# Five engines' written-out orders and the PSUM bank numbers replaced; partial maxima in two buffers

## The reference

```
h   = group_norm(x, 8 groups)
out = softmax(q k^T / sqrt(128)) v          # layer 0: one head of 128, 1024 x 1024
x   = x + proj(out)                         # t: tokens x 128
n   = layer_norm(t)
a   = softmax(sq sk^T / 4)                  # layer 1: 8 heads of 16, 1024 x 1024 each
ret = a @ rv (2 retrievers)                 # then a softmax over the 2 retrievers picks
t   = t + mix(ret) @ w_out
t   = t + layer_norm(t) @ dequant(qidx, scales)^T @ W^T
```

## Time and profile before

| | |
|---|---|
| median of 3 runs | 5282.57 us (5280.07 to 5285.5) |
| the profiled execution's own time | 5286.65 us |
| its span, first to last instruction | 5284.9 us |
| granted TensorE clock, mean | 0.971 |
| TensorE busy (matmuls) | 4855.4 us, 92% |
| GpSimd busy | 4245.3 us, 80% |
| VectorE busy | 3929.6 us, 74% |
| ScalarE busy | 3329.0 us, 63% |

### The profile page before, as it was taken

One profiled execution on the slowest core, in us unless ns is written; L12 is line 12 of the kernel. 1 busy time (PEld: TensorE's weight loads), 2 busy tenths in 40 slices (PEclk: granted clock), 3 DMA queues, 4 the chain that ended last, 5 costly groups with the idle time before them and its releaser, 6 DMA issues.

```text
span 5284.9 us, 102244 instructions
## 1 busy us (share of the span) xinstructions
PE 4855.4 (92%) x29838; PEld 2544.0 (48%) x29838; DVE 3929.6 (74%) x8176; ACT 3329.0 (63%) x6657; POOL 4245.3 (80%) x1173
## 2 busy tenths in 40 slices
...
GB/s 18 41 41 33 40 34 36 42 41 33 38 36 42 37 41 33 39 36 43 36 41 33 41 33 45 34 41 33 41 33 45 33 41 33 41 33 45 29 37 5
DMA packets 92849, 192.46 MB, mean 36 GB/s; under 512 B 16744, under 2 KB 50920, under 8 KB 92400
## 3 DMA queue, kind: packets, MB, share of 16 engines
...
...
## 4 chain that ended last, share of the span: by engine, by line
PE 58%; issue 18%; POOL 8%; ACT 7%; DVE 6%; ACTq 0%; DMA 0%; POOLq 0%; SPq 0%; DVEq 0%
PE ps_u L798 12%; PE ps_bank L749 8%; PE ps_bank L785 8%; POOL p_sum L639 8%; PE ps_bank L763 7%; ACT p L956 5%; DVE max_part L1057 3%; PE ps_bank L684 3%; PE ps_bank L673 3%; PE ps_bank L704 3%; PE ps_bank L735 2%; PE ps_bank L715 2%; PE ps_bank L807 2%; PE ps_bank L693 1%; PE ps_bank L738 1%
## 5 line engine op out<-in xcount | busy, mean ns | idle before, releaser
L639 POOL TENSOR_TENSOR p_sum<-p_sum,p 128x2048 f32<-128x2048 f32 x768 | 3500.6, 4558 | 176.5 <-ACT p L956 120.9
L1057 DVE TENSOR_REDUCE max_part<-ps_bank 128x1 f32<-128x512 f32 x4096 | 2615.0, 683 | 887.7 <-PE ps_bank L763 871.8
L956 ACT ACTIVATE p<-ps_bank 128x512 f32<-128x512 f32 x4096 | 2220.0, 601 | 1137.2 <-PE ps_bank L785 1111.8
L639 POOL TENSOR_TENSOR p_sum<-p 128x2048 f32<-128x2048 f32 x128 | 583.6, 4559 | 729.9 <-ACT den_sb L967 663.2
L798 PE MATMUL ps_u<-p,rv 128*32 128x512 f32 x8192 | 1050.3, 633 | 30.9 <-ACT p L956 30.9
L785 PE MATMUL ps_bank<-q_stack,k_stack 64*128 64x512 f32 x4096 | 952.9, 468 | 108.2 <-ACT p L956 57.7
L763 PE MATMUL ps_bank<-k_stack,q_stack 63*128 63x512 f32 x4096 | 935.8, 458 | 99.3 <-ACT p L956 66.6
L785 PEld LDWEIGHTS ps_bank<-q_stack,k_stack 64*128 64x128 f32 x4096 | 385.9, 186 | 722.8 <-issue 343.0
L763 PEld LDWEIGHTS ps_bank<-k_stack,q_stack 63*128 63x128 f32 x4096 | 390.0, 187 | 598.0 <-ACT p L956 238.4
L749 PE MATMUL ps_bank<-v,p 128*128 128x129 f32 x4096 | 521.8, 280 | 8.4 <-ACT p L956 7.0
L749 PEld LDWEIGHTS ps_bank<-v,p 128*128 128x128 f32 x4096 | 477.2, 191 | 85.2 <-issue 44.0
...
## 6 DMA issues: line engine op xcount, KB each, us to landing
...
k_stack<-k_lo SPq DMA_DIRECT2D x128, 128.0 KB, 2.7
q_stack<-q_lo SPq DMA_DIRECT2D x128, 128.0 KB, 2.8
...
```

What stands on the lines that cost most here:

```text
L639: pool.tensor_tensor(p_sum[:, :, :], before, p1[:, step % ring, :, :], ALU.add)\
L956: act.activation(p1[:, step % ring, n, :], bank_of("scores", index // 2, n % 2), ACT.Exp, scale=scale1)\
L1057: dve.tensor_reduce(max_part1[:, i, n, half:half + 1], bank_of("max1", index // 2, side), AXIS.X, ALU.max)\
```

## The change

All five lists are replaced. The entries are the same, one for one; their sequence, some images ahead and all bank numbers differ. Between two `den` entries TensorE's list holds:

| quarter | before | after |
|---|---|---|
| A | 31 pairs in 16 unbroken runs, 4 values, 3 value0, 7 score0, 2 result | 33 pairs in 15 runs, 4 values, 1 value0, 7 score0, 1 result |
| B | 33 pairs in 15 runs, 5 values, 4 value0, 1 score0, 2 q0, 2 k0 | 31 pairs in 12 runs, 4 values, 4 value0, 1 score0, 2 q0, 1 k0, 1 result |
| C | 33 pairs in 12 runs, 4 values, 8 max0, 2 v0, q1, k1, rqkv | 33 pairs in 11 runs, 5 values, 8 max0, 1 v0, q1, k1, rqkv, 1 k0, 2 max_rows0, 2 score0 |
| D | 31 pairs in 12 runs, 3 values, 1 value0, 8 score0, 2 max_rows0 | 31 pairs in 12 runs, 3 values, 3 value0, 6 score0, 1 v0 |

(What is not named is the same in both.) `x_tokens`, `value0.0` to `value0.2` and `score0.7` are now done two images ahead in place of one, `load` three in place of two, and 36 of VectorE's entries and 7 of ScalarE's one image further ahead. `max_part1` has two halves, taken in turn by phase, and VectorE's first `max0` of an image and first `max1` of a phase each begin with one more wait, on its own earlier `max0_last` or `max1_last`. The diff, cut (of TensorE's list quarter C and the ends stand here):

```diff
 PE_ORDER = """
-score0.7@1/1 max1.18@0/32 scores.1@0/04 max1.19@0/56 scores.2@0/13 max1.20@0/02 scores.3@0/45 x_tokens.0@1/1
...
-max1.52@0/62 scores.35@0/31 k0.0@2/5 max1.53@0/40 k0.1@2/6 scores.36@0/23 values.8@0 den.1@0/1 max1.54@0/40
-scores.37@0/56 ln1_channels.0@1/2 max1.55@0/31 ln1_channels.1@1/4 turn_den.1@0/5 turn_u.1@0/0 max0.0@2/26
-rqkv.0@1/3 scores.38@0/41 rqkv.1@1/5 q1.0@1/3 rqkv.2@1/4 k1.0@1/1 max1.56@0/25 scores.39@0/64 q1.1@1/0 k1.1@1/3
-max0.1@2/62 max1.57@0/41 values.9@0 max1.58@0/50 scores.40@0/64 max1.59@0/31 scores.41@0/26 max1.60@0/54
-scores.42@0/02 max1.61@0/36 scores.43@0/01 max1.62@0/25 max0.2@2/04 values.10@0 max0.3@2/13 max1.63@0/60
-scores.44@0/24 scores.45@0/51 scores.46@0/26 max0.4@2/43 max_rows1.3@0/5 scores.47@0/01 max0.5@2/42 max1.0@1/53
-max1.1@1/60 values.11@0 scores.48@0/14 max1.2@1/52 max0.6@2/36 scores.49@0/01 max1.3@1/54 scores.50@0/30
-max1.4@1/21 v0.0@2/6 max0.7@2/53 v0.1@2/4 scores.51@0/02 max1.5@1/16 scores.52@0/53 max1.6@1/40 values.12@0
-den.2@0/1 scores.53@0/26 max1.7@1/54 max_rows0.0@2/3 turn_den.2@0/0 max_rows0.1@2/1 turn_u.2@0/2 scores.54@0/56
...
-scores.62@0/32 score0.6@2/4 scores.63@0/61 max1.16@1/05 scores.0@1/32 max1.17@1/46 values.15@0
+den.3@-1/0 scores.3@0/45 max1.24@0/31 scores.4@0/26 turn_den.3@-1/0 turn_u.3@-1/4 scores.5@0/35 scores.6@0/12
...
+value0.7@1/0 result.1@-1/5 q0.0@2/4 q0.1@2/2 max1.54@0/13 scores.35@0/65 den.1@0/0 max1.55@0/42 values.8@0
+turn_den.1@0/6 k0.1@2/1 ln1_channels.0@1/5 turn_u.1@0/3 scores.36@0/04 ln1_channels.1@1/6 q1.0@1/2 max0.0@2/50
+rqkv.0@1/6 rqkv.1@1/4 rqkv.2@1/1 q1.1@1/5 max0.1@2/63 scores.37@0/41 scores.38@0/20 scores.39@0/64 max1.56@0/51
+max1.57@0/32 k1.0@1/0 k1.1@1/5 scores.40@0/61 max1.58@0/43 values.9@0 max1.59@0/20 max1.60@0/65 scores.41@0/14
+scores.42@0/32 max1.61@0/10 scores.43@0/46 scores.44@0/35 max1.62@0/24 max1.63@0/16 values.10@0 max0.2@2/03
+max0.3@2/25 max_rows1.3@0/4 max0.4@2/16 v0.0@2/0 max0.5@2/34 scores.45@0/25 scores.46@0/01 scores.47@0/62
+max1.0@1/35 max0.6@2/04 scores.48@0/13 scores.49@0/62 max0.7@2/01 values.11@0 max_rows0.0@2/4 max_rows0.1@2/3
+scores.50@0/56 scores.51@0/20 max1.1@1/14 score0.0@2/3 max1.2@1/56 max1.3@1/12 score0.1@2/4 max1.4@1/03
+max1.5@1/56 values.12@0 max1.6@1/14 scores.52@0/20 den.2@0/3 scores.53@0/56 max1.7@1/21 v0.1@2/0 turn_den.2@0/3
...
+max1.19@1/62 scores.0@1/51 scores.1@1/43 values.15@0 max1.20@1/51 scores.2@1/43 score0.6@2/6 score0.7@2/2
+max1.21@1/43 max1.22@1/05 max1.23@1/16 value0.0@2/2 value0.1@2/4 value0.2@2/3
...
 ACT_ORDER = """
...
+scores.0@1 scores.1@1 scores.2@1 scores.3@1 gate.2@0 evict_u.3@0 scores.4@1 scores.5@1 score0.6@2 score0.7@2
...
 DVE_ORDER = """
...
+max1_last.0@1 max1.32@1 max1.33@1 max1.34@1 max1.35@1 max1.36@1 max1.37@1 gate_arg.2@0 max1.38@1 max1.39@1
+retrieve.2@0 max1.40@1 max1.41@1 max1.42@1 max1.43@1 max1.44@1 max1.45@1 max1.46@1 max1.47@1 value0.0@2
...
 POOL_ORDER = """
-add.1@0 add.2@0 add.3@0 add.4@0 add.5@0 ln2_rstd.0@-1 add.6@0 add.7@0 add.9@0 add.10@0 add.11@0 add.12@0
-add.13@0 add.14@0 norm_rstd.0@2 add.15@0 ln1_rstd.0@1 add.17@0 add.18@0 add.19@0 add.20@0 add.21@0 add.22@0
+add.1@0 add.2@0 add.3@0 add.4@0 ln2_rstd.0@-1 add.5@0 add.6@0 add.7@0 add.9@0 add.10@0 add.11@0 add.12@0
+add.13@0 norm_rstd.0@2 add.14@0 add.15@0 ln1_rstd.0@1 add.17@0 add.18@0 add.19@0 add.20@0 add.21@0 add.22@0
 add.23@0 add.25@0 add.26@0 add.27@0 add.28@0 add.29@0 add.30@0 add.31@0
 """
 
 SP_ORDER = """
-take_rqk.0@0 rows.1@0 store.0@-1 load.0@2 take.0@0 rows.2@0 hold.0@1 stack.0@1 rows.3@0 rows.0@1 stack.1@1
+take_rqk.0@0 rows.1@0 rows.2@0 take.0@0 store.0@-1 stack.0@1 rows.3@0 hold.0@1 rows.0@1 load.0@3 stack.1@1
 """
 
 
@@ -355,7 +355,7 @@
         max_part0 = sb("max_part0", [P, tiles, halves])
         max_cols0 = sb("max_cols0", [P, tiles, P])
         max_row0 = sb("max_row0", [P, tokens], F32R)
-        max_part1 = sb("max_part1", [P, tiles_per_half, GROUP, halves])
+        max_part1 = sb("max_part1", [P, 2, tiles_per_half, GROUP, halves])
         max_cols1 = sb("max_cols1", [P, tiles_per_half, P])
         mixed = sb("mixed", [P, tiles, P])
         out_sb = sb("out_sb", [P, tokens])
@@ -1039,6 +1039,8 @@
 
                 def max0(b, index):
                     i, half = divmod(index, halves)
+                    if index == 0:
+                        wait(dve, max0_ready, 1 * b)
                     dve.wait_ge(filled["max0"], halves * tiles * b + index + 1)
                     dve.tensor_reduce(max_part0[:, i, half:half + 1], bank_of("max0", i, half), AXIS.X, ALU.max)\
                        .then_inc(maxed0, 1)
@@ -1051,16 +1053,19 @@
 
                 def max1(b, index):
                     phase, use = divmod(index, uses_per_phase)
+                    if use == 0:
+                        wait(dve, max1_ready, phases * b + phase - 1)
                     i, two, half, side = use // (GROUP * halves), use // (2 * halves) % 2, use // 2 % halves, use % 2
                     n = 2 * two + side
                     dve.wait_ge(max1_filled[side], maxima // 2 * b + index // 2 + 1)
-                    dve.tensor_reduce(max_part1[:, i, n, half:half + 1], bank_of("max1", index // 2, side), AXIS.X, ALU.max)\
+                    dve.tensor_reduce(max_part1[:, phase % 2, i, n, half:half + 1], bank_of("max1", index // 2, side),
+                                      AXIS.X, ALU.max)\
                        .then_inc(maxed1, 1)
 
                 def max1_last(b, phase):
                     wait(dve, filled["max_rows1"], phases * b + phase)
                     dve.wait_ge(maxed1, uses_per_phase * (phases * b + phase + 1))
-                    dve.tensor_reduce(max_cols1[:, :, 0:GROUP], max_part1[:, :, :, :], AXIS.X, ALU.max,
+                    dve.tensor_reduce(max_cols1[:, :, 0:GROUP], max_part1[:, phase % 2, :, :, :], AXIS.X, ALU.max,
                                       negate=True).then_inc(max1_ready, 1)
 
                 def x_tokens(b, half):
```

More of the change, by code:

```diff
@@ L43 @@
-out1.0@-1/2 score0.9@1/4 out1.1@-1/0 max1.31@0/15 scores.12@0/63 values.2@0 scores.13@0/42 score0.10@1/6
-scores.14@0/30 scores.15@0/14 score0.11@1/2 max_rows1.1@0/6 max1.32@0/53 max1.33@0/01 score0.12@1/5
-ln2_channels.0@-1/6 values.3@0 scores.16@0/34 max1.34@0/01 ln2_channels.1@-1/2 ffn.0@-1/6 score0.13@1/5
-scores.17@0/30 max1.35@0/41 result.0@-1/2 ffn.1@-1/6 scores.18@0/53 max1.36@0/40 score0.14@1/1 result.1@-1/2
-scores.19@0/65 max1.37@0/43 den.0@0/0 scores.20@0/12 max1.38@0/64 values.4@0 scores.21@0/53 max1.39@0/01
@@ L48 @@
-score0.15@1/6 turn_den.0@0/2 turn_u.0@0/4 scores.22@0/50 max1.40@0/31 scores.23@0/62 value0.4@1/5 max1.41@0/06
-scores.24@0/32 values.5@0 max1.42@0/14 scores.25@0/30 value0.5@1/2 max1.43@0/56 scores.26@0/13 max1.44@0/40
-max1.45@0/21 scores.27@0/53 value0.6@1/6 max1.46@0/54 scores.28@0/30 values.6@0 max1.47@0/21 scores.29@0/63
-value0.7@1/5 norm_mean.0@2/0 scores.30@0/46 norm_var.0@2/3 max_rows1.2@0/2 scores.31@0/10 max1.48@0/45
-max1.49@0/63 values.7@0 scores.32@0/21 max1.50@0/40 scores.33@0/56 q0.0@2/3 max1.51@0/21 q0.1@2/4 scores.34@0/50
@@ L63 @@
[L63 to L65 removed]
+den.3@-1/0 scores.3@0/45 max1.24@0/31 scores.4@0/26 turn_den.3@-1/0 turn_u.3@-1/4 scores.5@0/35 scores.6@0/12
+values.0@0 scores.7@0/60 max1.25@0/35 max1.26@0/12 value0.3@1/6 mixed_channels.0@-1/3 mixed_channels.1@-1/0
@@ new lines @@
+max1.27@0/45 values.1@0 max1.28@0/12 max1.29@0/30 scores.8@0/64 out1.0@-1/5 scores.9@0/16 scores.10@0/24
+out1.1@-1/3 score0.8@1/0 score0.9@1/1 max1.30@0/62 max1.31@0/45 score0.10@1/0 score0.11@1/3 scores.11@0/16
+scores.12@0/20 scores.13@0/43 max_rows1.1@0/5 scores.14@0/16 values.2@0 scores.15@0/20 max1.32@0/54 max1.33@0/31
+score0.12@1/6 max1.34@0/25 max1.35@0/04 values.3@0 ln2_channels.0@-1/3 scores.16@0/61 scores.17@0/25
+ln2_channels.1@-1/0 ffn.0@-1/4 scores.18@0/36 ffn.1@-1/0 result.0@-1/1 max1.36@0/42 max1.37@0/53 scores.19@0/06
```

94 lines of the change are left out of this document (47 added, 47 removed).

## The result

The kernel after takes 5032.55 us (median of 4 runs, 5030.68 to 5035.51), the kernel before 5283.17 us (4 runs, 5280.07 to 5285.5) beside it: ratio 0.9526, 95% interval [0.951, 0.9543]. That is 250.6 us less, where 144 were forecast. The direction came out and so did the shift of work between the quarters; the size did not.

What follows compares the result with a forecast made beforehand. The bound was taken to change hands by quarter: TensorE's work with its waits, GpSimd's additions in D. 4.8 us an image over 30 turns gave 144 us, 5286.65 - 144 - 4.1 = 5139 us; range of 8 in 10: 5040 to 5240.

Steps and rivals of the forecast that it cites:

- TensorE's work: Priced work between dens: A 40.1 to 36.0, B 36.2 to 32.6, C 33.4 to 37.9, D 29.8 to 31.4 us.
- A taken 37.4, C 43.8, D 34.3: Forecast lengths in us of quarters A, C and D, from TensorE's work, waits and GpSimd's bounds.
- the bound of 37.1: Quarter A can't be shorter than GpSimd's 34.3 + 2.1 (`ln2_rstd`) + 0.7 (`add.1` waits for `scores.3`) us.
- B: 32.6 and waits of 5.3 + 1.0 - 1.0 + 0.7 ... taken 37.0: Quarter B: new work plus old waits changed by single edits, less GpSimd's slack; 34.6 to 38.6 us.
- the rest was lost: Quarters with work below GpSimd's 34.3 us lose the difference; D lost 4.5 us and will lose 2.9.
- The banks, 14.7 against 14.5: Shortfall in us between a bank's return and next use, summed over A to D, old against new: scarcity unchanged.
- an image loses 1.0 us in the mean: Mean loss to falls of TensorE's granted clock, seen after the gap in quarter B at a `values` entry.
- Rival 4: The clock: two more falls to half clock an image cost at most 102 us, about 5210 us; chance 0.06.
- The last full turn ... gains nothing: The last full turn, 156.3 us, is paced by GpSimd at clock 0.80, so only 30 turns gain.
- Other edits at nothing: VectorE's added waits, `max_part1`'s second buffer, longer leads and ScalarE's `evict_u.3` taken as 0, the last within 0 to 2 us.
- Rival 1: New order hides nearly all waits, every quarter at its bound: turn 147.1 us, time 4977 us; chance 0.15.
- rival 2: Slower: GpSimd's late start in C and bank waits add up, C 49.2 us, time 5298 us; chance 0.11.

Runs made afterwards that it cites:

- x6: Kernel after, six of a phase's seven GpSimd additions on half of the columns: 4981.14 us, ratio 0.943 to the kernel before.
- x2: Kernel before, `norm_mean` and `norm_var` earlier on TensorE, `norm_rstd` ahead of `add.14`, ScalarE's `norm_var.0` ahead of `scores.60`: 5271.46 us, ratio 0.9957.
- x9: Kernel before with four useless matmuls in `max_rows1.2`'s bank ahead of its wait for VectorE, in quarter B: 5367.22 us, ratio 1.0147.
- x13: x5 with two useless matmuls in `max_rows1.2`'s bank ahead of its wait for VectorE: 5243.56 us, ratio 0.9932 to the kernel before.
- x15: x5 with one useless matmul in `max_rows1.2`'s bank ahead of its wait for VectorE: 5245.03 us, ratio 0.9935 to the kernel before.
- x5: Kernel before with the earlier norm entries of x2 and also `ln1_rstd.0` ahead of `add.15` on GpSimd: 5235.73 us, ratio 0.9909.
- x7: Kernel before, six of a phase's seven GpSimd additions on half of the columns: 5188.6 us, ratio 0.9825.
- x4: Kernel before with `value0.1` moved from behind `den.3` to ahead of it, VectorE's copy with it: 5280.29 us, ratio 0.9983.
- x1: The edits of code alone, with all five lists and banks of the kernel before: 5287.78 us, ratio 0.9995.

## Why the prediction was wrong

The points go in the order of its own steps.

- **TensorE's work:** the table of work between dens is what the quarters follow. A's 4.1 us are all work; C's 4.5 more show as 3.4. Right.
- **A taken 37.4, C 43.8, D 34.3:** measured 37.86, 42.94, 34.38, the three together 0.3 us less than taken. The late start of `add.18` was off by 0.2 us. The numbers were right, but the bounds named with them do not set A or C: both stay as they are with GpSimd's additions halved (x6). A kept its 1.9 us of waits, where a fall of 0.5 to 1.2 was reckoned with and the bound of 37.1 made up for it by luck.
- **"B: 32.6 and waits of 5.3 + 1.0 - 1.0 + 0.7 ... taken 37.0": this step failed.** B is 34.81 and its waits 2.2, where 37.0 - 32.6 = 4.4 were taken. The forecast carried the old waits over as a sum, moved by single edits. But the longest were one delay with three causes, each hidden by the others: `h` late, `ln1_rstd` late with ScalarE's queue behind it, and a half-clock `values.7`. x2 and x9 take one away each and B stays at 41.4 to 41.6; in x13 and x15 all three are gone and B is 1.8 us shorter, in x5 in every other image. The new lists avoid all three: the wait for `h` is 0.44 us, B has no clock fall in any middle image, and ScalarE's four `ln1_apply` stand behind `den.1` in place of among `scores.69` to `.72` (TensorE's `ln1_channels.0` starts 4.6 us behind `den.1` where it was 1.6). The other 1.3 us of waits were not undone one by one, and their cause stays open; the wait for `h` is not in them, as x13 has none. B cost the forecast 29 x 2.2 = 64 us.
- **D: "the rest was lost":** the number held by luck, for a wrong reason. D's 4.5 us were bank waits (x7, x4). New D has 1.6 more work and 1.5 less waits; with short additions it is 33.66 (x6), so GpSimd sets its last 0.7 us and TensorE would need nearly as long.
- **The banks, 14.7 against 14.5:** the sum of shortfalls said no change in waits. C and D lost 2.6 us of them, so as a forecast of the sum of waits the reckoning failed. Banks and order can't be told apart here: neither the new order with the old numbers nor the reverse was run. Nor were the lists of single engines.
- **The clock "an image loses 1.0 us in the mean":** taken as unchanged; most of it went, 22.9 of 29 us. The loss of 1.0 us was not the fall at `values.7` of the earlier trace rows, which cost nothing there, but those behind the wait for `h` and at `values.10`. Rival 4 looked for more falls only.
- **"The last full turn ... gains nothing":** the last two turns gave 29.2 us in place of 4.8. The first two cost 13 us where 0, within 8, was said; why they do was not tested.
- **Other edits at nothing:** right (x1; the bound of 0.1 us for a wait of VectorE's had no row, and x1 shows no cost at all). ScalarE's wait at `evict_u` fell, from 115.7 to 57.7 us in all.

The extra 112 us of the profiled executions are then: quarters 75, clock falls 23, last turns 24, fill and end 10 the other way.

Rival 1 (every quarter at its bound, 4977 us) was nearer in B, where it is reached, and in the time (56 us off, the forecast 106), and wrong in C. Of rival 2's mechanism half is there: GpSimd does start late in C, but sets nothing.
